# Attention in a four-layer transformer kernel: steps of one batch regrouped into units of one, two or four batches

## The reference, cut to what matters

```python
q, k, v = x @ Wq, x @ Wk, x @ Wv                      # per batch, 16 query heads, one k and one v
s[b, h] = q[b, h] @ k[b].T + bias[h] + key_mask[b]    # 512 x 512, causal: keys after the query are left out
p = softmax over the keys and the null key of s[b, h]
out[b, h] = p @ v[b]
```

## Time and profile before

| | |
|---|---|
| median of 3 runs | 2393.82 us (2392.82 to 2397.09) |
| the profiled execution | 2392.7 us |
| its span, first to last instruction | 2390.2 us |
| TensorE busy | 2071.5 us, 87% of the span |
| VectorE busy | 1118.4 us, 47% |
| ScalarE busy | 995.8 us, 42% |
| GpSimd busy | 589.3 us, 25% |
| mean granted TensorE clock | 0.928 |

### The profile page before, as it was taken

How to read it: one execution, slowest core, us unless ns; L and a number is a source line. 1 busy time by engine, 2 the same in 40 slices (tenths; PEclk the granted TensorE clock), 3 DMA queues, 4 the chain that set the end, 5 groups by cost and what they waited for, 6 DMA issues and landing times. The chain is left out here.

```text
span 2390.2 us, 47281 instructions
## 1 busy us (share of the span) xinstructions
PE 2071.5 (87%) x16272; PEld 1454.0 (61%) x16273; DVE 1118.4 (47%) x3373; ACT 995.8 (42%) x2622; POOL 589.3 (25%) x970
## 2 busy tenths in 40 slices
PE   6899999787999996899967765996889999959994
PEld 3477777654777775566644544883557776736663
DVE  5388882354888823201043336106568884321122
ACT  2388871155887721111113221213567783112221
POOL 2022120176111115211132332015811111321111
PEclk9999999998999997899968985997989999979997
DMA  2274422002533121422132332641010003131113
GB/s 80 77 217 132 142 66 93 0 1 62 151 93 92 55 72 40 141 99 99 54 105 92 126 104 96 203 139 36 0 48 20 20 11 142 36 123 46 44 44 114
DMA packets 157135, 197.91 MB, mean 83 GB/s; under 512 B 15315, under 2 KB 130223, under 8 KB 156941
## 3 DMA queue, kind: packets, MB, share of 16 engines
q1 hardware_dynamic: 145228, 169.09, 22.7%
q0 software_dynamic: 11712, 26.26, 3.1%
HBM read 120.60 MB, written 88.90 MB: 88 GB/s over the span
## 5 line engine op out<-in xcount | busy, mean ns | idle before, releaser
L938 ACT ACTIVATE att_pr<-all_h,att_nmax 128x128 f32<-128x128 f32 (+3 forms) x768 | 422.1, 552 | 93.2 <-DVE att_nmax L894 92.0
L996 PEld LDWEIGHTS att_t_ps<-all_ident,att_pr 64*128 64x128 f32 x3840 | 184.0, 139 | 108.6 <-issue 43.3
L996 PE MATMUL att_t_ps<-all_ident,att_pr 64*128 64x64 f32 x3840 | 188.5, 224 | 10.9 <-DVE att_pt L902 10.1
L874 POOL COPY att_rexp<-att_rinv 128x512 f32<-128x512 f32 x96 | 58.6, 610 | 515.7 <-DVE att_rinv L906 515.7
L1164 PE MATMUL out_y_ps<-outw_wo,mem_qt 128*128 128x256 f32 x768 | 179.2, 387 | 0.0
L902 DVE COPY att_pt<-att_t_ps 128x256 f32<-128x256 f32 (+3 forms) x240 | 177.3, 739 | 1.0 <-PE att_t_ps L996 1.0
L1786 PE MATMUL exp_f_h_ps<-exp_f_xs_t,cw_f_w 128*128 128x512 f32 (+1 forms) x512 | 172.5, 496 | 1.5 <-DVE exp_f_xs_t L1823 1.5
L1798 PE MATMUL exp_f_y_ps<-cw_f_w,exp_f_hid 128*128 128x256 f32 x768 | 168.4, 379 | 0.0
L1164 PEld LDWEIGHTS out_y_ps<-outw_wo,mem_qt 128*128 128x128 f32 x768 | 144.5, 193 | 25.4 <-issue 6.8
L1798 PEld LDWEIGHTS exp_f_y_ps<-cw_f_w,exp_f_hid 128*128 128x128 f32 x768 | 144.8, 190 | 19.5 <-issue 0.5
L1853 ACT ACTIVATE exp_f_hid<-exp_f_h_ps 128x512 f32<-128x512 f32 (+1 forms) x128 | 62.3, 490 | 222.2 <-PE exp_f_h_ps L1786 222.2
(11 more groups left out here) (395 smaller groups left out, 3886.1 us busy)
## 6 DMA issues: line engine op xcount, KB each, us to landing
sorted_c<-all_zero SPq DMA_DIRECT2D x8, 2056.0 KB, 13.1
sorted_f<-all_zero SPq DMA_DIRECT2D x8, 2056.0 KB, 11.3
cw_f_w<-in_L_ffn_w_dram SPq DMA_DIRECT2D x16, 1024.0 KB, 8.1
cw_f_w<-in_L_ffn_W_dram SPq DMA_DIRECT2D x16, 1024.0 KB, 8.5
com_f_rows<-expert_f SPq DMA_DIRECT2D x20, 512.0 KB, 6.9
band<-rev SPq DMA_DIRECT2D x2, 4096.0 KB, 18.6
att_bias<-band SPq DMA_DIRECT2D x32, 256.0 KB, 3.1
til_c_xs<-sorted_c SPq DMA_DIRECT2D x40, 128.5 KB, 2.1
```

The lines of the kernel that those rows point to most:

```text
L874: pool.tensor_copy(rexp[:], group_ap(rinv, G).unsqueeze(3).to_broadcast([P, B, 2, DH])).then_inc(rexp_ready, 1)
L938: nc.scalar.activation(pr[p % 4][:, hh, 0:n], sc[p % 4][:, hh, 0:n], ACT.Exp, scale=-1.0, bias=nmax[:, b, q, h:h + 1], accum_out=rsum[:, b ...
L996: last = nc.tensor.transpose(t_ps[e % 2][:, n, (q + 1) * hh + kb, :], pr[p % 4][d, hh, P * kb:P * (kb + 1)], c.ident[d, d])
```

## The change

The step becomes a unit of several batches. `TOGETHER = (4, 2, 1, 1)` says how many for each query block: the 128-key block takes its four batches at once, the 256-key block two, the two others one. A pair has 1 + 4 + 2 + 4 = 11 units instead of 16 steps, a call 88 instead of 128. The loops of the engines keep their shape and their distances, now in units: `scores(u + 2)`, `turn(u - 1)`, `values(u - 4)` and so on. The events of a group hang on its last unit (`group_after`). `rb_sb` gets a second buffer. `item` counts the single exponentials and row passes, which are as many as before.

```diff
+    TOGETHER = (4, 2, 1, 1)
     NG = HP * QT
-    NP = NG * B
+    units = [(B * (QT * i + j) + b, i, q, b, TOGETHER[q]) for i in range(HP) for j, q in enumerate(ORDER) for b in range(0, B, TOGETHER[q])]
+    NU = len(units)
+    last_of = [max(u for u in range(NU) if units[u][0] // B == G) for G in range(NG)]
+    group_after = {u: G for G, u in enumerate(last_of)}
+    turns = []
+    for u in range(NU + 3):
+        if u < NU:
+            turns.append(("unit", u))
+        if u - 2 in group_after:
+            turns.append(("sums", group_after[u - 2]))
+    turn_number = {turn: e for e, turn in enumerate(turns)}
...
-        rb_sb = m.sb("rb_sb", [P, B, P])
+        rb_sb = [m.sb(f"rb_sb{n}", [P, B, P]) for n in range(2)]
...
-        def taken_by_vector(p):
+        def taken_by_vector(u):
-            return steps[p][1] == 0 or p % 2 == 1
+            _, _, q, b, n = units[u]
+            return q == 0 or b // n % 2 == 1
...
             # largest (VectorE)
                 for hh in range(2):
                     h = 2 * i + hh
-                    dve.wait_ge(s_ready, 2 * p + hh + 1)
-                    if p >= 4:
-                        dve.wait_ge(p_ready, 2 * (p - 4) + hh + 1)
+                    dve.wait_ge(s_ready, 2 * u + hh + 1)
+                    if u >= 4:
+                        dve.wait_ge(p_ready, items(u - 4, hh))
+                    for k in range(n):
+                        at = slice(keys * k, keys * (k + 1))
+                        nc.vector.tensor_tensor_reduce(sc[u % 4][:, hh, at], s_ps[(2 * u + hh) % 3][:, at], bias_ap(i, q, hh), -1.0,
+                                                       c.nsn[:, b + k, q, h:h + 1], ALU.add, ALU.min,
+                                                       nmax[:, b + k, q, h:h + 1]).then_inc(s_read, 1)
...
             # the loop of VectorE
-                if p % B == 0 and p > B:
-                    put_out(p // B - 2)
-                if 2 <= p < NP + 2 and taken_by_vector(p - 2):
-                    take_pt(p - 2)
-                if p % B == 1 and p > B:
-                    invert(p // B - 1)
+                if u - 5 in group_after:
+                    put_out(group_after[u - 5])
+                if 2 <= u < NU + 2 and taken_by_vector(u - 2):
+                    take_pt(u - 2)
+                if u - 2 in group_after:
+                    invert(group_after[u - 2])
...
             # the loop of ScalarE
+            for u in range(NU + 4):
+                if u < NU:
+                    exponentials(u)
+                if u in group_after:
+                    null_keys(group_after[u])
+                if 2 <= u < NU + 2 and not taken_by_vector(u - 2):
+                    take_pt(u - 2)
+                if u - 4 in group_after:
+                    take_rb(group_after[u - 4])
...
             # scores (TensorE)
+                    bank = 2 * u + hh
+                    if bank >= 3:
+                        pe.wait_ge(s_read, items((bank - 3) // 2, (bank - 3) % 2))
+                    nc.tensor.matmul(s_ps[bank % 3][:, 0:keys * n].rearrange("p (b n) -> p b n", b=n), c.ones_b[d, :], c.kmask[d, b:b + n, 0:keys],
+                                     start=True, stop=False)
+                for k in range(n):
+                    tok = slice(S * (b + k) + P * q, S * (b + k) + P * (q + 1))
+                    for hh in range(2):
+                        d = slice(DH * hh, DH * (hh + 1))
+                        last = nc.tensor.matmul(s_ps[(2 * u + hh) % 3][:, keys * k:keys * (k + 1)], c.qt[d, i, tok], c.kt[d, b + k, 0:keys],
+                                                start=False, stop=(k == n - 1))
+                        if k == n - 1:
+                            last.then_inc(s_ready, 1)
...
             # the loop of TensorE
+            for u in range(NU + 4):
+                if u + 2 < NU:
+                    scores(u + 2)
+                if 1 <= u <= NU:
+                    turn(u - 1)
+                if u - 3 in group_after:
+                    turn_sums(group_after[u - 3])
+                if u >= 4:
+                    values(u - 4)
```

More of the change, by code:

```diff
@@ L879, in _, with largest @@
         def _(dve):
[L880 to L883, removed]
+            def largest(u):
+                first, i, q, b, n = units[u]
+                keys = P * (q + 1)
+                if b == 0:
                     if causal_select:
-                        dve.wait_ge(bias_ready, 2 * (p // B + 1))
-                    elif p % ROUND == 0:
+                        dve.wait_ge(bias_ready, 2 * (first // B + 1))
+                    elif first % ROUND == 0:
                         dve.wait_ge(bias_loaded[i % 2][0], 32 * (i // 2 + 1))
@@ L929, in _, with exponentials @@
         def _(a):
-            def exponentials(p):
-                i, q, b = steps[p]
-                n = P * (q + 1)
+            def exponentials(u):
+                first, i, q, b, n = units[u]
+                keys = P * (q + 1)
                 for hh in range(2):
                     h = 2 * i + hh
[L935 to L939, removed]
+                    for k in range(n):
+                        a.wait_ge(s_read, item(u, hh, k))
+                        if u >= 4 and hh == 0 and k == 0:
+                            a.wait_ge(turned, 2 * (turn_of(u - 4) + 1))
+                        at = slice(keys * k, keys * (k + 1))
+                        nc.scalar.activation(pr[u % 4][:, hh, at], sc[u % 4][:, hh, at], ACT.Exp, scale=-1.0, bias=nmax[:, b + k, q, h:h + 1],
+                                             accum_out=rsum[:, b + k, q, h:h + 1]).then_inc(p_ready, 1)
             def null_keys(G):
@@ L954, in take_rb @@
                 a.wait_ge(turned, 2 * (e + 1))
[L955 to L967, removed]
+                if G >= 2:
+                    a.wait_ge(out_ready, G - 1)
@@ L969, in _, with scores @@
         @block.tensor
         def _(pe):
[L971 to L974, removed]
+            def scores(u):
+                first, i, q, b, n = units[u]
+                keys = P * (q + 1)
                 for hh in range(2):
                     d = slice(DH * hh, DH * (hh + 1))
[L977 to L984, removed]
@@ L989, in turn @@
+            def turn(u):
+                _, _, q, _, n = units[u]
+                e = turn_of(u)
                 if e >= 2:
@@ L1009, in turn_sums, with values @@
                             last.then_inc(turned, 1)
-            def values(p):
-                _, q, b = steps[p]
-                e = turn_of(p)
+            def values(u):
+                first, _, q, b, n = units[u]
+                e = turn_of(u)
                 pe.wait_ge(t_copied[e % 2], e // 2 + 1)
[L1015 to L1020, removed]
+                if b == 0 and u:
+                    pe.wait_ge(out_ready, first // B)
+                for k in range(n):
+                    for kb in range(q + 1):
+                        for hh in range(2):
+                            block = (q + 1) * (n * hh + k) + kb
+                            last = nc.tensor.matmul(o_ps[DH * hh:DH * (hh + 1), b + k, :], c.v[:, QT * (b + k) + kb, :],
+                                                    pt[u % 4][:, P * block:P * (block + 1)], start=(kb == 0), stop=(kb == q))
                 last.then_inc(pv_done, 1)
```

80 lines of the change are left out of this document (42 added, 38 removed).

## The result

The changed kernel takes 2450.27 us (median of 4 runs, 2446.31 to 2457.97), the kernel before on the same chip 2395.4 us. The ratio is 1.0234, 95% interval 1.0206 to 1.0262: 55 us slower. The direction was forecast, the size was not: 2425 us in a range of 2396 to 2450, so the time lies just above the upper end. The profiled execution is the longest of the four, 2457.97 us, 65.3 us over the one of before.

A forecast was written before the change was run, and what follows sets the result against it. TensorE was taken as the bound. A pair at 32.9 us against 31.44 gave +30 us, first pairs -5, layer 0's selects +7.5: +32 on 2392.7, about 2425 us, range 2396 to 2450.

The forecast's parts named there:

- TensorE's own work, 28.4 us a pair: Scores 11.04, turns 5.90, sums 1.04, values 10.45 us per pair of heads, if no engine ever waited.
- Rival 3: The merged blocks don't shrink on TensorE, waits as forecast: 2449 us; chance 0.10.
- rival 2: Full gain: nothing waits, 28.4 us a pair, -72 us, 2322 us; chance 0.02.
- (a): Before turn of unit 0 (128-key block): late null key delays ScalarE's copy; chain 5.71 us, TensorE waits 2.26 us.
- Rivals 1 and 5: 1: null key not in the way, 2375 us, chance 0.12; 5: gains and waits cancel, within 5 us of now, 0.07.
- (b): Turn of unit 9 (block 2) waits 0.53 us for VectorE's copy behind the 8 row passes of unit 0.
- (c): Turn of unit 3 (block 3) waits 0.95 us for VectorE's copy behind four passes of unit 5 and `put_out`.
- (d): Turned sums of block 3's group wait 0.69 us for ScalarE's copy of unit 5, behind `null_keys` of block 1's group.
- The pair and its sum: 28.4 us of work plus 4.4 of waits: 32.9 us a pair against 31.44; whole-kernel sum +32 us.
- A rule of the skill against this change: Frequent short TensorE idles can make the clock swing; by the row at 102 to 104 us, priced at nothing.
- rival 4: Clock falls to 1.2 GHz at each 2.3 us gap: +84 us, near 2510 us; chance 0.03.
- The first pairs: First pair of each attention lacks two waits and has less waiting after the bias lands: -1.7 us each, -5 us.

The follow-up runs named there:

- e6: Kernel after with the null key's subtraction early for 128-key and 256-key groups, and ScalarE's and VectorE's copies swapped for 512-key and 384-key blocks; 2355.48 us, ratio 0.9784.
- e1: Kernel after with GpSimd's null-key subtraction for the 128-key group issued before its wait for the previous group's inverse; 2390.04 us, ratio 0.9948.
- e5: Kernel after with the null key's subtraction issued early for both the 128-key and 256-key groups; 2371.24 us, ratio 0.9854.
- e8: Kernel after with five added repeats of mask matmuls that change no output, filling TensorE's gap in each pair but the first; 2441.39 us, ratio 1.0139.
- e7: Kernel after with ScalarE's copy of the transposes put ahead of the null exponential in its list; 2426.24 us, ratio 1.0073.

## Why the prediction was right and where it failed

- **TensorE's own work, 28.4 us a pair.** Right as far as the runs reach: e6 comes within 0.7 of it, and no run is free of waits. The values block of unit 0 takes 1.02 us, as one block of the 512-key kind does. Rival 3 is out, and so is rival 2. The scores of unit 0 were put at 1.2 us and take 1.12 (680.21 to 681.33).
- **(a), the null key.** Right in place and size: 5.69 us against 5.71 for the chain; for the wait 2.08 in the idle column and 2.3 by e1 (33.03 to 30.73), against 2.26. Rivals 1 and 5 are out.
- **(b), turn of unit 9.** 0.49 against 0.53 us in the idle column above.
- **(c), turn of unit 3.** 0.81 against 0.95, in the row of the kernel after that waits for VectorE's copy:

```profile
667.99 0.71 PE L1030 MATMUL att_t_ps<-all_ident,att_pr 64*128 64x64 f32 x16 [0.81 <-DVE att_pt L928]
...
676.48 0.46 PE L1041 MATMUL att_t_ps<-all_ident,att_rexp 64*128 64x64 f32 x8 [0.48 <-ACT att_pt L978]
```

- **(d), the turned sums.** The second of these rows: 0.48 against 0.69. Taking its cause away (e5) gave back 0.71, the forecast, though the idle column shows less.
- **The pair and its sum.** 33.03 against 32.9 us; in layer 0 34.2, against 33.9. Without the falls of the clock (e8) the three attentions are 36.6 us longer than before; the prediction's sum was 32. e8's ratio, put on the 2395.4 us of the kernel before, gives 2429 us, and the forecast was 2425. This part was the whole of the forecast, and it holds.
- **The failed step: the clock.** Under "A rule of the skill against this change" I read from one row, 102 to 104 us at 1.00, that a gap of 2.3 us "does not show a lower clock here" and priced the clock at nothing; rival 4, whose mechanism is what happened, got 3 in 100. The falls cost 24.6 us in the profiled execution, where rival 4 said 84: not every gap lowered the clock (16 of 21), and a fall cost 1.5 us and not 4. The row was read too short, and it holds no gap of 2.3 us: it has the end of one of 1.66 us and the start of one of 3.47. That longer gap and the stretches right behind the row in the kernel before:

```profile
106.97 0.28 PE L980 MATMUL att_s_ps<-mem0k_kmask,all_ones_b 64*128 64x128 bf16 x1 [3.47 <-DVE att_nmax L894]
```

```profile
104.00:106.00 2.00, 0.00 (x0) 0.00 (x0) 0.00 (x0) 0.20 (x1) 0.02 (x1) 0.84 0.62 185
106.00:108.00 2.00, 0.90 (x6) 0.53 (x6) 0.83 (x5) 0.88 (x4) 0.52 (x2) 0.50 1.11 357
```

The clock falls there too, once TensorE has been idle: the mean is 0.84 in the stretch that the gap fills, and 0.50 behind it. So this trace had no gap near 2.3 us to judge by. That the measured time lies only 0.3 us above the range is chance: the upper end stood for blocks that don't shrink, which did not happen.

The passage of the Trainium skill that I weighed (TensorE: Matmul & The Clock Gate, A second HAM failure mode: psum-queue depth-cycling) speaks of frequent short idles. The traces here do not bear that out: e7 and e8 have many waits of 0.2 to 1.1 us, and the granted clock is 1.00 (640 to 865 and 640 to 870 us). The section before it on the same page of the Trainium skill, HAM oscillation, describes one long wait per round of a loop, after which each round starts at the low clock; the kernel after agrees with that in kind, with a wait of 2.1 to 2.6 us and the low clock in 16 of 21 rounds, not in each.

- **The first pairs.** Put at -1.7 us each, -5 together; e8 against before gives -0.5, -2.5 and -3.9, -6.9 together, and the kernel after -0.5, -0.2 and -3.9, -4.6 together. That the sum comes near is in part luck: how long the low clock lasts at the start of an attention differs between the traces and moved layer 1's first pair by 2.4 us.

## What to carry to other kernels

When steps are merged, list for each engine what stands right behind every instruction that waits for another engine, and ask whether its releaser moved by an index: here a 0.2 us subtraction held a copy, and the copy held TensorE. Add chains up from start to start in rows; waits found so were right to 0.2 us. Then ask of every wait that comes to 2 us on TensorE what the clock does behind it, in the stretches after the gap.

## What was not expected of the hardware

- A wait of TensorE of 2.1 us (2.6 in layer 0) in a stage that is otherwise about 90% busy was followed by a granted clock of 0.50 in 16 of 21 cases, and by 1.00 in the other five, with the same instructions around it. With the gap filled down to 0.6 us (1.1 in layer 0, e8) it was none of 21.
- Added matmuls that compute nothing new made the attentions 27 us shorter (e8 against after), 2.4 of them by the clock at the start of one attention.
- Eight repeats of the mask matmul for the two heads took 2.6 us (the gap of 2.1 and 0.5 over it), not the 1.8 expected from 0.22 us each. The repeats of one head start 0.22 us apart; the second head's nine matmuls stand behind the first head's nine in the list, start 1.1 us after them and overlap them only in part.
